# Product 4 of the W_base stage by seven inner products over two pairs, in an adaLN and feed-forward kernel

## The chip, the cores and the metric

The kernel runs on one core of a Trainium2 chip. The metric is device time in microseconds (us), the median of the runs. Engines: PE is TensorE (matmuls), DVE is VectorE, ACT is ScalarE, POOL is GpSimd, SP is SyncE (here it only issues transfers).

## The reference

For each of 16 batches of 512 tokens by 1024 features:

```
q_emb = relu(cond @ W3 + b3)
n, v_sum = tokens, sum of x over tokens
c = relu(((n * x + v_sum) * q_emb) @ W2 + b2)                # stage 1, 1024 x 1024
base   = c @ W_base + b_base                                 # stage 2, 1024 x 1024
shared = (c @ A_s) @ B_s                                     # rank 16
gates  = softmax(c @ W_router + b_router), the best 2 of 6 kept
routed = sum over e of gate_e * (c @ A_r[e]) @ B_r[e]        # rank 16 each
out = x + base + shared + routed
```

Everything is float32. Each matmul operand is split into a rounded part (hi) and the rest (lo), both float32r, and each product is three matmuls: hi by hi, hi by lo, lo by hi (`three`, L2390 to L2394).

## The kernel before, in words

Two batches make a pair, eight pairs in all; a pair's 1024 x 1024 by 1024 x (2 x 512) product is one block product of 2 x 2 by 2 x 2 blocks, done by Strassen-Winograd's seven block products, numbered 0 to 6, instead of eight. Both stages do that: `g` 0 to 7 are the pairs of the first stage (W2), `g` 8 to 15 those of the second (W_base), where p = g - 8. A block product `group(g, n, j)` for j = 0 to 3 has four groups, one for each 128 output features; a group is 4 x 3 = 12 matmuls into one PSUM bank. In stage 2 the rank-16 parts join as `low_rank`: three matmuls more at the end of a group of products 4, 5 and 6. Their four output blocks are C11, C12, C22, C21; C11 is made of products 0 and 1, and its low-rank rows have a place of their own: `low_rank_c11` (L2610) writes them to a bank, and DVE adds the bank (`c11_add_low`, L2178).

In pairs 2 to 7 of both stages product 1 isn't done pair by pair. Two neighbouring pairs have the same weight block there, so the two blocks of data are put side by side, and that wider product is again cut in two each way and done by seven inner products (`inner(e, m)`, L2548: 12 matmuls each, m = 0 to 6) instead of two block products of 48 matmuls. They are done in the even pair (g = 2, 4, 6 and 10, 12, 14, the list `QUADS`); the odd pair only adds what was kept for it (`partner`). Inner weight sets are quarters of W and their sums, split in hi and lo. There is no room to keep them on the core; they are written once to HBM by way of a staging buffer of two slots, and each is loaded again, 512 KB, before its inner product into one of two slots (`inner_w`).

How a weight set is made: ACT rounds it (`inner_weight_high(c)`, L1026; c counts the sets, 0 to 6 for W2, 7 to 13 for W_base, and after the change 14 to 20), having waited until set c - 2 is stored; DVE makes the rest (`inner_weight_low(c)`, L1813); four sums on DVE make the sets 3 to 6 of a kind (`inner_weight_sums`, L1818); POOL's queue stores it (`store_weights`, L720). For W_base this is done in the last pair before the first even one, g = 9 (`SECOND - 1`).

What sets the order: it is written out by hand. Each engine has one instruction stream, waits are on semaphores, and an engine never passes a waiting instruction. POOL's stream in stage 2 is: the seven stores; then for each even pair the first two weight sets (`begin`), the other pair's data (`load_partner`, two loads of 512 KB), and the five sets m = 2 to 6 (`stream`), each waiting until inner product m - 2 is done. PE's order in an even pair (`even`, L2637): four groups of product 0 and three of product 2, each followed by an inner product, and the last group of product 2; then products 3 (with `low_rank_c11` after each group), 4, 5 and 6. ACT rounds operands (`high`, L827) and copies banks (`copy_p0`, `copy_u2`, `copy_u4`); DVE makes the low parts (`low`, L1511), the operand sums (`t1` to `t4`) and the outputs (`add_bank`, L1594).

## Time and profile before

| | |
|---|---|
| time of the runs | 1394.6 us (median of 3; 1394.54 to 1394.91) |
| span of the profiled execution | 1392.4 us |
| the median less that span | 2.2 us (no time of the profiled execution itself beside its span is given) |
| PE busy | 1388.2 us, 100% of the span, 6105 matmuls |
| DVE, ACT, POOL busy | 71%, 46%, 4% |
| granted PE clock | 1.00 in every slice |
| transfers | 237.8 MB, 171 GB/s on average |

A profiled matmul is shown with a duration of 0.39 us, but matmuls overlap: what counts is the distance from the start of one to the start of the next. In the same way DVE's and ACT's instructions overlap a little, so a chain of them goes by distances between starts. The number in brackets at the end of a timeline row is how long the engine stood idle before it, and what it waited for.

### The profile page before, as it was taken

To read this page: it belongs to the slowest core of one execution; us is meant where nothing else is said; L and a number is where in the kernel's file an instruction comes from. 1 tells how busy PE (TensorE), PEld (TensorE's weight loads), DVE (VectorE), ACT (ScalarE), POOL (GpSimd) and SP (SyncE) were. 2 spreads that over 40 slices of the span, in tenths; PEclk is the share of its full clock that TensorE was granted. 3 is DMA by queue.
4 is the path that set the end of the run, shared out by engine and by line. 5 is a ranking of instruction groups with operands and counts; after the bars stand their busy time and mean duration, and the time that the engine had idled before them with its cause. 6 is when DMAs were issued, how large, how long until landed. Compare 5 with 4: busy or idle time off the path is not lost.

```text
span 1392.4 us, 18247 instructions
## 1 busy us (share of the span) xinstructions
PE 1388.2 (100%) x6105; PEld 1142.9 (82%) x6105; DVE 986.5 (71%) x1648; ACT 644.2 (46%) x1190; POOL 60.7 (4%) x136
## 2 busy tenths in 40 slices
PE   9999999999999999999999999999999999999999
PEld 6888888888888888888888888888888888888887
DVE  6987777676786757768889667766667656586663
ACT  7774756657465564655544232431314313243130
POOL 3000110000000000000000001000000000000000
PEclk9999999999999999999999999999999999999999
DMA  8243836445264452546836549556463665635542
GB/s 318 75 168 113 263 122 182 156 122 165 62 184 153 122 165 61 171 130 211 285 92 195 212 132 342 176 190 226 146 239 114 203 213 167 218 107 175 211 155 87
DMA packets 146429, 237.78 MB, mean 171 GB/s; under 512 B 39872, under 2 KB 40128, under 8 KB 146336
## 3 DMA queue, kind: packets, MB, share of 16 engines
q1 hardware_dynamic: 135680, 199.75, 43.6%
q0 software_dynamic: 9792, 35.66, 8.3%
q10 hardware_dynamic: 864, 1.22, 0.2%
...
## 4 chain that ended last, share of the span: by engine, by line
PE 100%; DVE 0%; DVEq 0%; issue 0%
PE ps L2392 33%; PE ps L2393 33%; PE ps L2394 33%; PE ps L2403 1%; PE ps L2418 0%; PE ps L2412 0%; DVE buf L2385 0%; DVEq L59 0%; DVE zeros L1708 0%
## 5 line engine op out<-in xcount | busy, mean ns | idle before, releaser
L2392 PE MATMUL ps<-act_hi,w_hi 128*128 128x512 f32 x1600 | 623.0, 389 | 0.0
L2393 PE MATMUL ps<-act_lo,w_hi 128*128 128x512 f32 x1600 | 622.8, 389 | 0.0
L2394 PE MATMUL ps<-act_hi,w_lo 128*128 128x512 f32 x1600 | 622.8, 389 | 0.0
L2392 PEld LDWEIGHTS ps<-act_hi,w_hi 128*128 128x128 f32 x1600 | 300.4, 188 | 63.1 <-DVE act_lo L1520 0.9
L2393 PEld LDWEIGHTS ps<-act_lo,w_hi 128*128 128x128 f32 x1600 | 300.4, 188 | 62.3
L2394 PEld LDWEIGHTS ps<-act_hi,w_lo 128*128 128x128 f32 x1600 | 300.4, 188 | 62.2
L854 ACT ACTIVATE act_hi<-src 128x512 fp32r<-128x512 f32 x232 | 140.5, 624 | 152.6 <-PE ps L2394 151.5
L1595 DVE SCALAR_TENSOR_TENSOR buf<-ps,bb_sb,buf 128x512 f32<-128x512 f32 x115 | 85.6, 748 | 125.6 <-PE ps L2394 100.7
L1527 DVE TENSOR_TENSOR act_lo<-src,act_hi 128x512 fp32r<-128x512 f32 x192 | 130.2, 685 | 23.8 <-ACT act_hi L854 23.6
L873 ACT ACTIVATE yhi<-buf 128x512 fp32r<-128x512 f32 x128 | 80.1, 626 | 81.3 <-PE ps L2394 80.9
L1595 DVE SCALAR_TENSOR_TENSOR buf<-ps,b_sb,buf 128x512 f32<-128x512 f32 x80 | 59.4, 748 | 43.8 <-PE ps L2394 43.7
L1520 DVE SCALAR_TENSOR_TENSOR act_lo<-src,shift,act_hi 128x512 fp32r<-128x512 f32 x104 | 76.6, 747 | 18.8 <-ACT act_hi L851 18.8
L851 ACT ACTIVATE act_hi<-src,shift 128x512 fp32r<-128x512 f32 x100 | 69.9, 715 | 11.4 <-PE ps L2394 9.4
L854 ACT ACTIVATE act_hi<-buf 128x512 fp32r<-128x512 f32 x64 | 39.0, 627 | 71.5 <-DVE buf L1560 61.7
L1650 DVE TENSOR_TENSOR buf_lo<-buf,yhi 128x512 fp32r<-128x512 f32 x64 | 43.4, 687 | 37.9 <-ACT yhi L873 37.8
L895 ACT ACTIVATE buf<-ps 128x512 f32<-128x512 f32 x64 | 37.5, 592 | 68.3 <-PE ps L2394 68.1
L906 ACT ACTIVATE buf<-ps 128x512 f32<-128x512 f32 x60 | 35.7, 596 | 70.7 <-PE ps L2394 70.6
L808 ACT ACTIVATE src<-src,qn 128x512 f32<-128x512 f32 x92 | 65.4, 711 | 2.8 <-DMA src<-in_xT 2.8
L2393 PE MATMUL ps<-act_lo,inner_w 128*128 128x512 f32 x168 | 65.4, 389 | 0.0
L2394 PE MATMUL ps<-act_hi,inner_w 128*128 128x512 f32 x168 | 65.4, 389 | 0.0
L2392 PE MATMUL ps<-act_hi,inner_w 128*128 128x512 f32 x168 | 65.4, 389 | 0.0
L1527 DVE TENSOR_TENSOR act_lo<-buf,act_hi 128x512 fp32r<-128x512 f32 x64 | 42.4, 685 | 19.0 <-ACT act_hi L854 18.9
...
## 6 DMA issues: line engine op xcount, KB each, us to landing
...
y_scratch<-buf SPq DMA_DIRECT2D x128, 256.0 KB, 3.1
src<-y_scratch SPq DMA_DIRECT2D x128, 256.0 KB, 5.2
...
```

The source lines that it names most:

```text
L808: nc.scalar.activation(src[:, t, :], src[:, t, :], ACT.Identity, scale=qn[:, H * HALF_OF[q] + k, 2 * i + BATCH_OF[q]:2 * i + BATCH_OF[q] + 1],
L851: nc.scalar.activation(act_hi[:, slot(g, n, k), :], source[:, t, :], ACT.Identity, bias=shift[:, t:t + 1]).then_inc(hi_done, 1)
L854: nc.scalar.activation(act_hi[:, slot(g, n, k), :], source[:, t, :], func).then_inc(hi_done, 1)
L873: nc.scalar.activation(yhi[:, (y_no(i, c, j) - 1) % 2, :], buf[:, j, :], func).then_inc(yhi_done, 1)
L895: nc.scalar.activation(buf2[:, j, :], ps[:, j, :], ACT.Copy).then_inc(u2_copied, 1)
L1520: nc.vector.scalar_tensor_tensor(act_lo[:, s, :], source, shift[:, t:t + 1], act_hi[:, s, :].bitcast(F32), ALU.add, ALU.subtract).then_inc ...
L1527: nc.vector.tensor_tensor(act_lo[:, s, :], source, act_hi[:, s, :].bitcast(F32), ALU.subtract).then_inc(lo_done, 1)
L1595: nc.vector.scalar_tensor_tensor(buf, ps[:, bank, :], bias, buf, ALU.add, ALU.add).then_inc(done, 1)
L1650: nc.vector.tensor_tensor(lo, y, hi, ALU.subtract).then_inc(ylo_done, 1)
L2392: nc.tensor.matmul(out, wh, a_h, start=start, stop=False, skip_group_check=onto)
L2393: nc.tensor.matmul(out, wh, a_l, start=False, stop=False, skip_group_check=onto)
L2394: return nc.tensor.matmul(out, wl, a_h, start=False, stop=stop, skip_group_check=onto)
```

## The change

- Product 4 of pairs 2 to 7 of stage 2 is done for two pairs at once, as product 1 is. Each even pair has two runs of seven inner products, r for product 1 and f for product 4; the weight sets of product 4 are a third kind (c = 14 to 20), stored and loaded as the others are. The raw quarters come from adding hi and lo of the W_base block that is on the core (`raw_four`).
- The low-rank rows of C11 (even pairs) and of C12 (both pairs) no longer ride on a group of product 4 or on a bank of their own: in an even pair inner products 1 and 5 of either run have six low-rank matmuls more, that accumulate in the inner product's banks (`with_low`); in an odd pair `low_rank_c12` adds three matmuls into the bank of each group of product 3, after ACT has copied it.
- C12 of the even pair is gathered in a new buffer (`acc4`), whose x rows SP loads ahead; product 4 of the odd pair waits in `partner4`, loaded by POOL.
- The orders of all engines in the even pairs are written anew, and in pair g = 9 and at the start of g = 10 the making of sets 14 to 20 is put in.

The diff, cut to its core:

```diff
+        def four_joined(g):
+
+            return g >= NP and joined(g)
+
+        RUNS = [(e_of, n_of) for e_of in range(len(QUADS)) for n_of in ((1, 4) if e_of >= EARLY else (1,))]
+        RUN = {key: r_of for r_of, key in enumerate(RUNS)}
+
...
-                if n_of != 1 or not joined(g_of):
+                if not (n_of == 1 and joined(g_of)) and not (n_of == 4 and four_joined(g_of)):
...
+            def load_x12(p):
+                for j in range(H):
+                    if p > 2:
+                        sp.wait_ge(buf1_stored[j], 16 * 2 * (NP + p - 1))
+                    else:
+                        sp.wait_ge(inner_w_lo, 3 * L2)
+                    sp.dma_start(acc4[:, j, :], xT[2 * p + 1, j]).then_inc(x12_loaded[j], 16)
...
+            def inner_weights(r, m):
+                e, n = RUNS[r]
+                c = L2 * r + m
+                kind = 2 if n == 4 else int(e >= EARLY)
                 if m < 2 and e in (0, EARLY):
-                    for r in range(2):
-                        pool.wait_ge(inner_w_stored[r], 16 * ((L2 * (late + 1) + 1 - r) // 2))
+                    weights_stored(kind)
                 if c >= 2:
                     pool.wait_ge(inner_done, 2 * (c - 1))
-                pool.dma_start(inner_w[:, c % 2], inner_dram[late, m]).then_inc(inner_w_loaded[c % 2], 16)
+                pool.dma_start(inner_w[:, c % 2], inner_dram[kind, m]).then_inc(inner_w_loaded[c % 2], 16)
+
+            def load_partner4(e):
+                g = QUADS[e] + 1
+                if e == EARLY:
+                    weights_stored(2)
+                for h in range(2):
+                    if e > EARLY:
+                        pool.wait_ge(c12_done, four(QUADS[e] - 1, 2 * h + 1))
+                    for k in (2 * h, 2 * h + 1):
+                        pool.wait_ge(buf3_stored[k], 16 * (g - NP + 1))
+                    pool.wait_ge(partner_loaded[h], other_loaded_no(RUN[e, 1]))
+                    pool.dma_start(partner4[:, 2 * h:2 * h + 2, :],
+                                   y_dram[2 * (g - NP) + 1, H + 2 * h:H + 2 * h + 2].rearrange("k p t -> p k t")
+                                   ).then_inc(partner_loaded[h], 16)
 
             def load_partner(e):
                 g = QUADS[e] + 1
...
                         for k in (2 * h, 2 * h + 1):
                             pool.wait_ge(buf2_stored[k], 16 * (g - NP + 1))
                         from_dram = y_dram[2 * (g - NP), H + 2 * h:H + 2 * h + 2]
+                        pool.wait_ge(partner_loaded[h], other_loaded_no(RUN[e, 1] - 1))
                     pool.dma_start(partner[:, 2 * h:2 * h + 2, :], from_dram.rearrange("k p t -> p k t")
...
             for e in range(EARLY, len(QUADS)):
-                begin(e)
+                begin(RUN[e, 1])
                 load_partner(e)
-                stream(e)
+                if e == EARLY:
+                    for c in range(2 * L2, 3 * L2):
+                        store_weights(c)
+                load_partner4(e)
+                stream(RUN[e, 1])
+                begin(RUN[e, 4])
+                stream(RUN[e, 4])
 
...
+                a_max(r)
+                inner_high(r, 0)
+                inner_high(r, 1)
+                if e == EARLY:
+                    inner_weight_high(3 * L2 - 2)
                 copy_p0(g, 0)
-                inner_high(e, 2)
+                lr_high_a(p)
+                inner_high(r, 2)
                 copy_p0(g, 1)
-                inner_high(e, 3)
                 copy_p0(g, 2)
-                inner_high(e, 4)
+                if e == EARLY:
+                    inner_weight_high(3 * L2 - 1)
                 for j in range(H):
                     high(g, 2, j)
+                a_max(f)
...
-                    if g == SECOND - 1 and j in (0, 2):
-                        inner_weight_high(L2 + 5 + j // 2)
-                if p < LAST:
-                    for j in range(H):
-                        high(g + 1, 0, j)
+                    if g == SECOND - 1 and j in (0, 1):
+                        inner_weight_high(L2 + 5 + j)
+                    elif g == SECOND - 1:
+                        inner_weight_high(2 * L2 + j - 2)
+                for j in range(H):
+                    high(g + 1, 0, j)
+                    if g == SECOND - 1 and j > 0:
...
+            def raw_four():
+
+                dve.wait_ge(bank_done, group_no(SECOND - 1, 4, H - 1))
+                for k in (0, 2):
+                    nc.vector.tensor_tensor(wl_raw[:, 4, k:k + 2, :], w_lo[:, 4, k:k + 2, :].bitcast(F32),
+                                            w_hi[:, 4, k:k + 2, :].bitcast(F32), ALU.add).then_inc(inner_w_sum, 1)
 
...
+                r, f = RUN[e, 1], RUN[e, 4]
+                inner_low(r, 0)
+                inner_t1(r)
+                inner_low(r, 1)
+                inner_t2(r)
+                if e == EARLY:
+                    inner_weight_low(3 * L2 - 2)
+                lr_low_a(p)
+                add_p0(r, 0)
+                inner_low(r, 2)
+                inner_t3(r)
+                add_p0(r, 1)
+                if e == EARLY:
+                    inner_weight_low(3 * L2 - 1)
+                add_p1(r, 0)
+                add_p1(r, 1)
...
+                if g == SECOND - 1:
+                    raw_four()
...
+                    if g == SECOND - 1 and j == 1:
+                        inner_weight_low(2 * L2 + 2)
+                        inner_weight_sums(2)
+                    elif g == SECOND - 1 and j > 1:
+                        inner_weight_low(2 * L2 + 1 + j)
...
+                with_low = e >= EARLY and m in (1, 5)
+                    inner_free(r, m, jt)
+                        s = inner_slot(r, m) + kk
+                                   act_hi[:, s, :], act_lo[:, s, :], kk == 0 and not onto, kk == 1 and not with_low,
+                                   onto)
+                    if not with_low:
+                        mm.then_inc(inner_done, 1)
+                if with_low:
+
+                    p = QUADS[e] - NP
+                    hi, lo = (ha_hi, ha_lo) if n == 1 else (hb_hi, hb_lo)
+                    pe.wait_ge(lr_lo_done, 3 * p + (2 if n == 1 else 3))
+                    for jt in range(2):
+                        j = jt + (2 if m == 5 else 0)
+                        cols = slice(j * P, (j + 1) * P)
+                        three(ps[:, B_BANKS[jt], :], low_hi[:, cols], low_lo[:, cols], hi[:, :], lo[:, :], False, True,
+                              onto).then_inc(inner_done, 1)
...
 
+            def low_rank_c12(p, j):
+
+                pe.wait_ge(u4_copied, four(NP + p, j))
+                if j == 0:
+                    pe.wait_ge(lr_lo_done, 3 * p + 3)
+                cols = slice(j * P, (j + 1) * P)
+                three(ps[:, j, :], low_hi[:, cols], low_lo[:, cols], hb_hi[:, :], hb_lo[:, :], False, True,
+                      True).then_inc(lr_done, 1)
...
+                r, f = RUN[e, 1], RUN[e, 4]
+                group(g, 0, 0)
+                inner(r, 0)
+                group(g, 0, 1)
+                group(g, 0, 2)
+                inner(r, 1)
+                group(g, 0, 3)
+                inner(r, 2)
+                group(g, 2, 0)
+                inner(r, 3)
+                group(g, 2, 1)
+                inner(r, 4)
+                group(g, 2, 2)
+                inner(r, 5)
+                inner(r, 6)
+                group(g, 2, 3)
+                for j in range(H):
+                    group(g, 3, j)
+                    inner(f, j)
+                for j in range(H):
+                    group(g, 5, j, (1, 3 * (g - NP) + 3, hb_hi, hb_lo))
+                    if j < H - 1:
+                        inner(f, H + j)
+
+            def odd(p):
+                g = NP + p
                 for j in range(H):
                     group(g, 0, j)
+                for j in range(H):
                     group(g, 2, j)
+                    low_rank_c11(p, j)
+                group(g, 3, 0)
+                group(g, 3, 1)
+                low_rank_c12(p, 0)
+                group(g, 3, 2)
+                low_rank_c12(p, 1)
+                group(g, 3, 3)
+                low_rank_c12(p, 2)
+                low_rank_c12(p, 3)
+                for j in range(H):
+                    group(g, 5, j, (1, 3 * p + 3, hb_hi, hb_lo))
```

Three places where the streams are different. First POOL, from the stores of the W_base weight sets to the first even pair (`staged_w`, in the changed kernel `staged_1`, is the staging buffer, `inner_scratch` its copy in HBM, `inner_w` the two slots that PE reads). Before:

```order
L722 DMA inner_scratch<-staged_w 128x1024 [waits inner_w_lo] x7
L733 DMA inner_w<-inner_scratch 128x1024 [waits inner_done,inner_w_stored1,inner_w_stored0] x2
L746 DMA partner<-y_scratch 128x2x512 [waits buf2_stored1,buf2_stored0]
L746 DMA partner<-y_scratch 128x2x512 [waits buf2_stored3,buf2_stored2]
L733 DMA inner_w<-inner_scratch 128x1024 [waits inner_done] x7
```

And now:

```order
L848 DMA inner_scratch<-staged_1 128x1024 [waits inner_w_lo] x7
L864 DMA inner_w<-inner_scratch 128x1024 [waits inner_done,inner_w_stored1,inner_w_stored0] x2
L892 DMA partner<-y_scratch 128x2x512 [waits partner_loaded0,buf2_stored1,buf2_stored0]
L892 DMA partner<-y_scratch 128x2x512 [waits partner_loaded1,buf2_stored3,buf2_stored2]
L848 DMA inner_scratch<-staged_4 128x1024 [waits inner_w_lo] x7
L876 DMA partner4<-y_scratch 128x2x512 [waits buf3_stored1,buf3_stored0,partner_loaded0,inner_w_stored1,inner_w_stored0]
L876 DMA partner4<-y_scratch 128x2x512 [waits partner_loaded1,buf3_stored3,buf3_stored2]
L864 DMA inner_w<-inner_scratch 128x1024 [waits inner_done] x5
L864 DMA inner_w<-inner_scratch 128x1024 [waits inner_done,inner_w_stored1,inner_w_stored0] x2
```

Between the loads for inner products 0 and 1 and the loads for 2 to 6 there now stand seven stores, each waiting for DVE, and two loads of `partner4`, the first of which waits until all stores have landed.

Second ACT, from the operands of product 6 in pair g = 9 to the first inner operand of g = 10 (`act_hi<-src 128x512` are operands of groups, `act_hi<-src 128x1024` those of inner products, `staged` the weight sets). Before:

```order
L854 ACTIVATE act_hi<-src 128x512 [waits op_used,t4_made]
L1348 ACTIVATE ha_hi<-hd 128x512 [waits lr_done,hd_made]
L854 ACTIVATE act_hi<-src 128x512 [waits op_used,t4_made]
L1034 ACTIVATE staged_w<-wl_raw 128x512 [waits inner_w_stored1,inner_w_sum,wl_loaded1]
L854 ACTIVATE act_hi<-src 128x512 [waits bank_done,t4_made]
L854 ACTIVATE act_hi<-src 128x512 [waits op_used,x_loaded0]
L854 ACTIVATE act_hi<-src 128x512 [waits op_used,x_loaded1]
L854 ACTIVATE act_hi<-src 128x512 [waits op_used,x_loaded2]
L854 ACTIVATE act_hi<-src 128x512 [waits bank_done,x_loaded3]
L1045 ACTIVATE src<-src 128x1024 [waits x_loaded13,x_loaded12]
L1103 ACTIVATE act_hi<-src 128x1024 [waits op_used,a_ready]
```

And now:

```order
L1193 ACTIVATE staged_1<-wl_raw 128x512 [waits inner_w_stored1,inner_w_sum,wl_loaded1]
L1010 ACTIVATE act_hi<-src 128x512 [waits op_used,t4_made]
L1193 ACTIVATE staged_4<-wl_raw 128x512 [waits inner_w_stored0,inner_w_sum]
L1010 ACTIVATE act_hi<-src 128x512 [waits bank_done,t4_made]
L1193 ACTIVATE staged_4<-wl_raw 128x512 [waits inner_w_stored1,inner_w_sum]
L1010 ACTIVATE act_hi<-src 128x512 [waits op_used,x_loaded0]
L1010 ACTIVATE act_hi<-src 128x512 [waits op_used,x_loaded1]
L1193 ACTIVATE staged_4<-wl_raw 128x512 [waits inner_w_stored0,inner_w_sum]
L1010 ACTIVATE act_hi<-src 128x512 [waits op_used,x_loaded2]
L1193 ACTIVATE staged_4<-wl_raw 128x512 [waits inner_w_stored1,inner_w_sum]
L1010 ACTIVATE act_hi<-src 128x512 [waits bank_done,x_loaded3]
L1193 ACTIVATE staged_4<-wl_raw 128x512 [waits inner_w_stored0,inner_w_sum]
```

Six rows for weight sets stand between operands that PE needs, each with a wait for a store (`inner_w_stored`); before it was one.

Third DVE, at the end of pair g = 9 and in the first even pair (`act_lo<-src,act_hi 128x512` are operands of groups). Before:

```order
L1527 TENSOR_TENSOR act_lo<-src,act_hi 128x512 [waits hi_done]
L1595 SCALAR_TENSOR_TENSOR buf2<-ps,bb_sb,buf2 128x512 [waits bank_done,u2_copied]
L1543 TENSOR_TENSOR src<-src 128x512 [waits x_loaded2,x_loaded10]
L1527 TENSOR_TENSOR act_lo<-src,act_hi 128x512 [waits hi_done]
L1595 SCALAR_TENSOR_TENSOR buf2<-ps,bb_sb,buf2 128x512 [waits bank_done,u2_copied]
L1543 TENSOR_TENSOR src<-src 128x512 [waits x_loaded3,x_loaded11]
L1595 SCALAR_TENSOR_TENSOR buf2<-ps,bb_sb,buf2 128x512 [waits bank_done,u2_copied]
L1920 TENSOR_TENSOR act_lo<-src,act_hi 128x1024 [waits inner_hi_done]
```

And now:

```order
L1765 TENSOR_TENSOR src<-src 128x512 [waits x_loaded1,x_loaded9]
L2037 TENSOR_TENSOR staged_4<-wl_raw,staged_4 128x512 [waits inner_w_hi]
L2053 TENSOR_TENSOR wl_raw<-wl_raw 128x2x256 [waits inner_w_lo,inner_w_sum]
L2054 TENSOR_TENSOR wl_raw<-wl_raw 128x2x256
L2056 TENSOR_TENSOR wl_raw<-wl_raw 128x2x256 [waits inner_w_sum]
L2058 TENSOR_TENSOR wl_raw<-wl_raw 128x2x256 [waits inner_w_sum]
L1749 TENSOR_TENSOR act_lo<-src,act_hi 128x512 [waits hi_done]
L1817 SCALAR_TENSOR_TENSOR buf2<-ps,bb_sb,buf2 128x512 [waits bank_done,u2_copied]
L1765 TENSOR_TENSOR src<-src 128x512 [waits x_loaded2,x_loaded10]
...
L2037 TENSOR_TENSOR staged_4<-wl_raw,staged_4 128x512 [waits inner_w_hi]
L1817 SCALAR_TENSOR_TENSOR buf2<-ps,bb_sb,buf2 128x512 [waits bank_done,u2_copied]
L2163 TENSOR_TENSOR act_lo<-src,act_hi 128x1024 [waits inner_hi_done]
```

A weight set and the four sums stand ahead of the third operand of product 0, and one more weight set ahead of the last C21 row of the pair before and the first inner operand.

## Rows read from the trace of the kernel before

**Rows 1.** Page, busy times; then the waits of PE over the span.

```profile
PE 1388.2 (100%) x6105; PEld 1142.9 (82%) x6105; DVE 986.5 (71%) x1648; ACT 644.2 (46%) x1190; POOL 60.7 (4%) x136
...
PE ps L2418 <- DVE zeros L1708: 1.2, 1, 1.2
```

**Rows 2.** Timeline of PE: start us, duration us, engine, line, operation.

```profile
1.17 3.52 PE L2418 MATMUL ps<-zeros 128*128 128x512 bf16 x9 [1.17 <-DVE zeros L1708]
...
902.30 0.39 PE L2392 MATMUL ps<-act_hi,w_hi 128*128 128x512 f32 x1
...
905.02 0.39 PE L2392 MATMUL ps<-act_hi,inner_w 128*128 128x512 f32 x1
...
918.62 0.39 PE L2392 MATMUL ps<-ha_hi,low_hi 128*128 128x512 f32 x1
```

**Rows 3.** Timeline of POOL around the start of pair g = 10.

```profile
854.18 0.53 POOL L722 DMA_DIRECT2D inner_scratch<-staged_w  x1 [2.59 <-DVE staged_w L1815]
860.17 0.53 POOL L722 DMA_DIRECT2D inner_scratch<-staged_w  x1 [5.45 <-DVE staged_w L1815]
868.52 1.07 POOL L733 DMA_DIRECT2D inner_w<-inner_scratch  x2 [7.82 <-DMA inner_scratch<-staged_w]
869.57 1.49 POOL L746 DMA_DIRECT2D partner<-y_scratch  x2
881.13 0.55 POOL L733 DMA_DIRECT2D inner_w<-inner_scratch  x1 [10.07 <-PE ps L2394]
```

**Rows 4.** Landing times: the stores at 854.18 and 860.17, all 14 stores.

```profile
DMA to landing us min/median/max: 6.2/6.2/6.2
...
DMA to landing us min/median/max: 7.6/7.6/7.6
...
DMA to landing us min/median/max: 3.2/5.3/7.7
```

**Rows 5.** Landing times of loads: inner_w at 868.5, partner at 869.6, all 42 inner_w.

```profile
DMA to landing us min/median/max: 4.5/5.2/5.9
...
DMA to landing us min/median/max: 7.2/7.6/7.9
...
DMA to landing us min/median/max: 3.6/3.8/5.9
```

**Rows 6.** Windows: busy time by engine, clock, DMA share, GB/s.

```profile
865.00:870.00 5.00, 5.00 (x24) 4.14 (x23) 3.38 (x6) 1.06 (x1) 1.48 (x3) 1.00 1.08 403
895.00:900.00 5.00, 5.00 (x23) 4.14 (x23) 3.87 (x7) 1.62 (x4) 0.53 (x1) 1.00 0.27 86
```

**Rows 7.** Timeline of ACT: a weight set, operand of product 6, copy after product 3.

```profile
856.49 0.63 ACT L1034 ACTIVATE staged_w<-wl_raw 128x512 fp32r<-128x512 f32 x1 [4.87 <-DMA inner_scratch<-staged_w]
857.03 0.62 ACT L854 ACTIVATE act_hi<-src 128x512 fp32r<-128x512 f32 x1
...
918.82 0.60 ACT L906 ACTIVATE buf<-ps 128x512 f32<-128x512 f32 x1 [1.08 <-PE ps L2394]
```

**Rows 8.** Timeline of DVE from the last weight sets to the first inner operands.

```profile
834.86 0.68 DVE L1821 TENSOR_TENSOR wl_raw<-wl_raw 128x512 f32<-128x512 f32 x1
...
837.52 0.68 DVE L1527 TENSOR_TENSOR act_lo<-src,act_hi 128x512 fp32r<-128x512 f32 x1
...
852.55 0.74 DVE L1595 SCALAR_TENSOR_TENSOR buf<-ps,bb_sb,buf 128x512 f32<-128x512 f32 x1
853.21 0.68 DVE L1815 TENSOR_TENSOR staged_w<-wl_raw,staged_w 128x512 fp32r<-128x512 f32 x1
853.81 0.68 DVE L1527 TENSOR_TENSOR act_lo<-src,act_hi 128x512 fp32r<-128x512 f32 x1
...
875.37 0.75 DVE L1595 SCALAR_TENSOR_TENSOR buf<-ps,bb_sb,buf 128x512 f32<-128x512 f32 x1 [2.05 <-PE ps L2394]
876.03 1.22 DVE L1920 TENSOR_TENSOR act_lo<-src,act_hi 128x1024 fp32r<-128x1024 f32 x1
877.17 1.22 DVE L1866 SCALAR_TENSOR_TENSOR partner<-partner,src 128x1024 f32<-128x1024 f32 x1
...
887.02 2.49 DVE L1560 SCALAR_TENSOR_TENSOR buf<-src 128x512 f32<-128x512 f32 x4
```

723 lines of the change are left out of this document (489 added, 234 removed).

## The prediction, written before the changed kernel had run

> **What bounds the kernel now.** I read the page's busy times and PE's waits first [rows 1]: PE is busy for 1388.2 of 1392.4 us, and its one wait with a releaser is 1.2 us at the start. PE never waits for an operand, a bank or a weight set, so every matmul removed is time saved, and every microsecond that the change makes PE wait is time lost. Then PE's timeline [rows 2]: the matmuls at 902.30 and 905.02 are the first ones of neighbouring blocks of twelve, so a matmul costs 2.72 / 12 = 0.2267 us and a block 2.72. The one at 902.30 starts the eleventh block of pair g = 10 (four groups and four inner products of product 0's part, group 0 of product 2, inner product 4 before it), so that pair begins at 902.30 - 10 x 2.72 = 875.1; the DVE row at 875.37, which waits for the last group of pair 9, agrees [rows 8]. The granted clock is 1.00 in all windows, of which two are shown [rows 6]. After that I read the stretch from 850 to 905, where the third kind of weight sets is now made: POOL [rows 3], landings [rows 4, 5], ACT [rows 7] and DVE [rows 8]. The reader should see there that DVE and ACT have gaps but that the transfers are full: DMA share 1.08 at 403 GB/s between 865 and 870, against 0.27 between 895 and 900 [rows 6].
>
> **Matmuls.** For two joined pairs, product 4 was 2 x 48 matmuls and 2 x 12 low-rank ones, 120. Now it is 7 x 12 = 84, 12 low-rank ones in the even pair (inner products 1 and 5 of run f) and 12 in the odd (low_rank_c12), 108. C11's twelve are as many as before. Three times 12 go: 36 x 0.2267 = -8.2 us. This term is sure, 0.6% of the time.
>
> **The weight sets of product 4, and where they are late.** Everything else depends on the hand-over from g = 9 to g = 10. POOL now issues the loads for inner products 0 and 1 and for partner, then seven stores, each after DVE has made its set, then (after all have landed) partner4, and only then the load for inner product 2. In the new PE order inner product 2 comes after g00, inner 0, g01, g02, inner 1 (18 matmuls) and g03 (gnj is group j of product n): 5 x 2.72 + 4.08 = 17.7 us into the pair, at 892.8 on the old time axis. When does its weight set land? I follow sets 12 to 20.
>
> Step 1. DVE's C12 row at 852.55 and the set at 853.21 [rows 8] are now parted by raw_four, two operations on 1024 columns (1.14 us each, the distance 876.03 to 877.17), and an operand; set 12 starts at 856.1, and its store is issued 0.97 later (853.21 to 854.18 [rows 3]). Landings there took 6.2 and 7.6 us [rows 4]: set 12 lands at about 864.0, and set 13, stored at 858.9, at 866.2. ACT rounds set 14 only then (it waits for set 12), and behind it stands the last operand of product 6, whose high part was made at 857.03 [rows 7] and is now made at 864.6; DVE's part ends at 865.9. PE wants it 11.6 us before g = 10 (a group with low rank is 15 matmuls, 3.4 us; four of them less three quarters of the first's 12), at 863.5: 2.4 late.
>
> Step 2. POOL waits for set 13 (866.2), needs 2.56 us for four loads (868.52 to 871.06 [rows 3]) and issues the store of set 14 at 868.8, behind 2 MB of loads of its own. Partner took 7.2 to 7.9 us in that place [rows 5]; I take 8: 876.9. Set 16 waits for that on ACT, with two operands of g = 10's product 0 behind it. DVE then makes set 16, the four sums (2.66 us, 834.86 to 837.52 [rows 8]) and the third operand: ready at 881.6, with set 17 and the fourth at 884.0, where PE wants it at 877.1 unshifted. 7.0 late.
>
> Step 3. Set 18, the last C21 row and the low part of the first inner operand come after it on DVE: ready at 887.9, where it was 877.2 (876.03 + 1.22) [rows 8] and wanted at 877.8. 10.1 late.
>
> Step 4. From the start of that low part (886.7) DVE needs, to set 20: four operations of 1.14, set 19 and a low-rank part (0.60 each, as 853.21 to 853.81), a bank (0.66, as 852.55 to 853.21), two of 1.14, a bank, and four t2 in 2.4: 11.8 us. Set 20 starts at 898.5, its store at 899.5. The x rows of acc4 (four loads of 256 KB) wait for the same set and go beside it. With the median of all stores, 5.3 [rows 4], it lands at 904.8; partner4's two issues take 1.5 [rows 3]; the load of set 2 is issued at 906.3 and takes 5.2 as the pair of loads at 868.5 did [rows 5]: 911.5 against 892.8, so D = 18.7 us late in all.
>
> Bounds of D. If every store lands in 3.2 and the load in 3.6 [rows 4, 5], steps 1 to 3 vanish in DVE's gaps and set 20 starts at 887.8: 888.8 + 3.2 + 1.5 + 3.6 = 897.1, D = 4.3. If all take 7.7 and 5.9, the first inner operand starts at 888.5 and D is 23.6. Nothing makes D less than 4.3 as long as POOL's stream stands as it does, for all the terms are in series. I take D = 17, between, near the upper side, since steps 1 and 2 lie in the full stretch and step 4 in the empty one.
>
> The page "DMA: Bandwidth & Descriptors" of the Trainium skill (section on the anatomy of a POOL-issued DMA) gives a fixed 2.0 us and bytes / 436e3 for one transfer, an estimate of 3.2 us for 512 KB; the shortest row agrees, the median of 5.3 doesn't. By that page alone D would be near the lower bound of 4.3 and the kernel 3 us faster, the low edge of rival 2 below; the landings under load decide for the rows.
>
> **PE after a long wait.** The trace shows PE slow only at its start: nine matmuls in 3.5 us, 0.38 each instead of 0.2267 [rows 2], 1.4 us lost, though the granted clock reads 1.00 there too. After the wait at inner product 2 (some 7 us) I add the same 1.4; the bounds are 0 and three times that, as there are several waits.
>
> The page "TensorE: Matmul & The Clock Gate" of the Trainium skill (Part 1) says that the array falls to 1.2 GHz when idle and that activity releases it; a stretch at half clock costs its own half. No row of this trace shows a fall.
>
> **The odd pairs.** In low_rank_c12 the fourth trio waits for ACT's copy of the bank that the group just before finished; only the third trio, 0.68 us, lies between. A copy starts 0.20 after a group's end (918.62 to 918.82) and lasts 0.60 [rows 2, 7]: at least 0.12 us of waiting, with the hand-over back to PE about 0.25, bounded by 0 and 0.5. Three odd pairs: +0.8.
>
> **The even pairs' new second half.** The first operand of run f is rounded after inner product 6, two copies, two operands and copy_u2; counting from the end of that product with 0.2 to start and ACT's starts 0.5 to 0.6 apart, DVE's part is ready 5.1 us after it where PE wants it at 5.4 (groups g23 and g30). DVE itself comes there with 13 operations and six wide ones after inner product 4, 14 us of 14.9. Nothing waits, by 0.3 us: I take 0, bounds 0 and 3 us per even pair. Behind it on DVE stand c12's banks, which PE wants 10 us later, so a small slip isn't passed on. SP's acc4 loads wait for set 20 with nothing behind them that is due before product 3. The two later even pairs have no weight sets to make, and partner4 waits only for the odd pair's C12 rows, done in product 6 and before inner product 2 by over 17 us.
>
> **Sum.** 1392.4 - 8.2 + 17.0 + 1.4 + 0.8 = 1403.4 of span. The runs' median is 2.2 above the profiled span: 1405.6 us, 0.8% slower.
>
> **Rivals.**
> 1. The sets are in time, and only the matmuls count: 1394.6 - 8.2 + 0.8 = 1387.2, faster. For it: DVE was idle 2.05 us before 875.37 [rows 8], and sets 14 to 18 could slip in. Against it: store, partner4 and load in series behind set 20 need 8.3 us even at the shortest landings, and PE leaves 4. It needs an order on POOL that isn't there. 9%.
> 2. Short landings: the stretch is emptier than before because DVE's own lateness spreads the transfers, D = 4.3 to 10 and no slow restart: 1394.6 - 8.2 + 0.8 + 7.5 = 1394.7, within 0.2%. For it: the median of inner_w is 3.8. Against: two of the three links lie behind other transfers. 12%.
> 3. The even pairs' second half waits too: if DVE's slack of 0.3 us is an error of one wide operation and hand-overs, each of three pairs loses 1 to 3 us, 1405.6 + 5 = 1410.6. It decides where run f's first operand is later than g30's end. 10%.
> 4. The sharp side of steps 1 to 3, D = 23.6 with a second slow restart: 1405.6 + 6.6 + 1.4 = 1413.6. 6%.
> The rest, 63%, is the forecast, with its own range of 1398 to 1411.
>
> **Chances.** A measurement of this kernel can tell 0.2%, 2.8 us, from no change. Faster (under 1391.8): rival 1 and the low edge of rival 2, 12%. Within: the rest of rival 2, 10%. Slower 78%. The range of 1391 to 1412 leaves out rival 1 and most of rival 4.
>
> **What would show it.** Right: PE matmuls 36 fewer; PE idle in one piece of 5 to 10 us before inner product 2 of g = 10, released by a load of inner_w; shorter waits for act_lo at the last operand of product 6 in g = 9 and at g00 and inner 0; POOL idle until a landing of inner_scratch just before partner4; waits of 0.1 to 0.5 us for ACT's copies in three odd pairs. The span from 910 to the end is then shorter by about 7 us than before. Wrong: POOL's load for inner product 2 issued before 889; a PE without waits at 892; or waits of over 1 us in pairs 12 and 14, which none of my terms has.

## The result, and the profile after

| | before | after |
|---|---|---|
| time of the runs | 1394.71 us (4 runs; 1394.54 to 1394.91) | 1412.28 us (4 runs; 1411.66 to 1414.27) |
| ratio | | 1.0126, 95% interval 1.0112 to 1.0141 |
| profiled execution: time, span | span 1392.4 us | 1414.27, 1412.4 us |
| PE matmuls | 6105 | 6069 |
| granted clock, mean | 1.00 | 0.992 |

The kernel is 1.3% slower, where 0.8% was forecast, and the time lies 0.3 us outside the range. The profile's busy line of the changed kernel (before: [rows 1]):

```profile
PE 1388.9 (98%) x6069; PEld 1139.6 (81%) x6069; DVE 1037.6 (73%) x1700; ACT 664.0 (47%) x1209; POOL 79.5 (6%) x170
```

36 matmuls fewer, as counted, and yet PE is busy 0.7 us longer. So there is more to find than waits. The waits of PE (us in total, times, longest), against the single 1.2 of [rows 1]:

```profile
PE ps L2760 <- issue: 8.7, 1, 8.7
PE ps L2760 <- DVE act_lo L1749: 8.5, 3, 7.2
PE ps L2760 <- DVE act_lo L2163: 2.0, 1, 2.0
PE ps L2786 <- DVE zeros L1930: 1.2, 1, 1.2
```

Five places stop PE, all at the hand-over from g = 9 to g = 10. PE's timeline there, which answers to [rows 2]:

```profile
864.45 0.50 PE L2760 MATMUL ps<-act_hi,w_hi 128*128 128x512 f32 x1 [0.46 <-DVE act_lo L1749]
...
884.93 0.80 PE L2760 MATMUL ps<-act_hi,w_hi 128*128 128x512 f32 x1 [7.25 <-DVE act_lo L1749]
...
887.40 0.79 PE L2760 MATMUL ps<-act_hi,w_hi 128*128 128x512 f32 x1 [0.81 <-DVE act_lo L1749]
...
891.05 0.80 PE L2760 MATMUL ps<-act_hi,inner_w 128*128 128x512 f32 x1 [2.01 <-DVE act_lo L2163]
...
917.06 0.77 PE L2760 MATMUL ps<-act_hi,inner_w 128*128 128x512 f32 x1 [8.68 <-issue]
...
921.04 0.63 PE L2760 MATMUL ps<-act_hi,inner_w 128*128 128x512 f32 x1
921.46 0.63 PE L2761 MATMUL ps<-act_lo,inner_w 128*128 128x512 f32 x1
```

The five rows with brackets are the last operand of product 6, g00's third and fourth operand, inner product 0 and inner product 2. Measured from start to start and less one matmul's 0.2267, they stop PE for 0.62, 7.40, 1.22, 2.41 and 8.84 us: 20.5 in all. The last has no engine as its releaser; the load issued at 910.62 (below) landed 6.3 us later, at 916.9, and that is what it waited for. The last two rows are 0.42 us apart where full speed is 0.2267: after the waits PE goes on at about half speed. The windows (columns: stretch, length, PE, PEld, DVE, ACT, POOL busy, granted clock, DMA share, GB/s), two of 10 us and then three short ones, against the 1.00 of [rows 6]:

```profile
880.00:890.00 10.00, 3.30 (x6) 1.67 (x6) 9.10 (x15) 5.88 (x8) 1.55 (x3) 0.59 0.43 156
...
910.00:920.00 10.00, 2.94 (x7) 2.42 (x8) 2.25 (x3) 1.48 (x3) 1.75 (x3) 0.63 0.63 210
...
882.00:884.90 2.90, 0.00 (x0) 0.00 (x0) 2.83 (x6) 1.15 (x2) 0.36 (x1) 0.50 0.51 184
...
895.40:898.00 2.60, 2.60 (x12) 2.09 (x11) 1.96 (x3) 1.06 (x1) 0.53 (x1) 0.98 0.59 213
...
914.00:917.00 3.00, 0.00 (x0) 0.00 (x0) 0.00 (x0) 0.00 (x0) 0.00 (x0) 0.50 0.95 318
```

The granted clock falls while PE waits: it is at 0.50, the 1.2 GHz level, in the last 2.9 us before g00's third operand and in the last 3 us before inner product 2, stays there for the first matmuls, and is back at the 2.4 GHz level some matmuls later (0.98 from 895.4 on). The matmuls that are further apart than 0.2267 without being a wait cost 7.0 us together: about 3.3 from 884.9 to 895.5, 2.8 from 917.1 to 923, and 0.84 in the odd pairs (below). The account is then -8.2 + 20.5 + 7.0 = +19.3, and the span grew by 20.0.

POOL, which answers to [rows 3]; the row at 870.69 is the store of set 14, the one at 903.77 that of set 20:

```profile
868.19 1.06 POOL L864 DMA_DIRECT2D inner_w<-inner_scratch  x2 [6.78 <-DMA inner_scratch<-staged]
869.24 1.49 POOL L892 DMA_DIRECT2D partner<-y_scratch  x2
870.69 0.59 POOL L848 DMA_DIRECT2D inner_scratch<-staged  x1
...
903.77 0.53 POOL L848 DMA_DIRECT2D inner_scratch<-staged  x1 [7.81 <-DVE staged L2037]
909.17 1.45 POOL L876 DMA_DIRECT2D partner<-y_scratch  x2 [4.88 <-DMA inner_scratch<-staged]
910.62 1.13 POOL L864 DMA_DIRECT2D inner_w<-inner_scratch  x2
```

and the landings of the store at 870.69 and of the two loads at 910.62 (before: [rows 4, 5]):

```profile
DMA to landing us min/median/max: 9.3/9.3/9.3
...
DMA to landing us min/median/max: 6.3/6.7/7.0
```

ACT's rounding of set 13, which waited for the store of set 11 (issued at 852.04, landed 7.0 us later), and of set 16, which waited for the store at 870.69 (compare [rows 7]):

```profile
859.10 0.63 ACT L1193 ACTIVATE staged<-wl_raw 128x512 fp32r<-128x512 f32 x1 [6.76 <-DMA inner_scratch<-staged]
...
880.07 0.63 ACT L1193 ACTIVATE staged<-wl_raw 128x512 fp32r<-128x512 f32 x1 [10.88 <-DMA inner_scratch<-staged]
```

and DVE (compare [rows 8]): g00's third operand, the first inner operand, inner product 2's own operand, set 20.

```profile
884.19 0.68 DVE L1749 TENSOR_TENSOR act_lo<-src,act_hi 128x512 fp32r<-128x512 f32 x1
...
889.78 1.21 DVE L2163 TENSOR_TENSOR act_lo<-src,act_hi 128x1024 fp32r<-128x1024 f32 x1
...
897.33 1.22 DVE L2163 TENSOR_TENSOR act_lo<-buf,act_hi 128x1024 fp32r<-128x1024 f32 x1 [0.64 <-ACT act_hi L1273]
...
902.77 0.69 DVE L2037 TENSOR_TENSOR staged<-wl_raw,staged 128x512 fp32r<-128x512 f32 x1
```

This is the chain as forecast, link by link; from the second link on each is later than forecast. From inner product 2 to the last matmul the new kernel needs 1408.95 - 917.06 = 491.9 us, 489.1 without the slow restart, where it was 1388.95 - 892.8 = 496.2: 7.1 shorter, about what the matmuls less the odd pairs' waits give (8.2 - 0.8 = 7.4).

### The profile page after: what moved, and what is told of

Same layout as the page of the kernel before. It is cut to its first block and busy times, and to the rows that moved or that the text cites. A ratio compares the mean times of both kernels' runs of the same rounds, so it can differ in the third digit from the quotient of the medians.

```text
span 1412.4 us, 18365 instructions
## 1 busy us (share of the span) xinstructions
PE 1388.9 (98%) x6069; PEld 1139.6 (81%) x6069; DVE 1037.6 (73%) x1700; ACT 664.0 (47%) x1209; POOL 79.5 (6%) x170
## 3 DMA queue, kind: packets, MB, share of 16 engines
q10 hardware_dynamic: 864, 1.22, 0.2%
## 5 line engine op out<-in xcount | busy, mean ns | idle before, releaser
L2760 PE MATMUL ps<-act_hi,w_hi 128*128 128x512 f32 x1504 | 586.5, 390 | 8.5 <-DVE act_lo L1749 8.5
L2761 PE MATMUL ps<-act_lo,w_hi 128*128 128x512 f32 x1504 | 585.6, 389 | 0.0
L2762 PE MATMUL ps<-act_hi,w_lo 128*128 128x512 f32 x1504 | 585.6, 389 | 0.0
L2760 PEld LDWEIGHTS ps<-act_hi,w_hi 128*128 128x128 f32 x1504 | 282.7, 188 | 69.4 <-DVE act_lo L1749 10.1
L2762 PEld LDWEIGHTS ps<-act_hi,w_lo 128*128 128x128 f32 x1504 | 282.7, 188 | 58.7
L1817 DVE SCALAR_TENSOR_TENSOR buf<-ps,bb_sb,buf 128x512 f32<-128x512 f32 x91 | 67.4, 748 | 64.7 <-PE ps L2762 61.0
L2760 PE MATMUL ps<-act_hi,inner_w 128*128 128x512 f32 x252 | 100.4, 398 | 10.7 <-issue 8.7
L2762 PE MATMUL ps<-act_hi,inner_w 128*128 128x512 f32 x252 | 99.8, 396 | 0.0
L2761 PE MATMUL ps<-act_lo,inner_w 128*128 128x512 f32 x252 | 99.7, 396 | 0.0
L1062 ACT ACTIVATE buf<-ps 128x512 f32<-128x512 f32 x60 | 35.7, 594 | 66.6 <-PE ps L2762 66.5
L2760 PEld LDWEIGHTS ps<-act_hi,inner_w 128*128 128x128 f32 x252 | 48.4, 192 | 22.3 <-issue 9.1
```

The source lines that it names most:

```text
L1062: nc.scalar.activation(buf3[:, j, :], ps[:, j, :], ACT.Copy).then_inc(u4_copied, 1)
L1817: nc.vector.scalar_tensor_tensor(buf, ps[:, bank, :], bias, buf, ALU.add, ALU.add).then_inc(done, 1)
L2760: nc.tensor.matmul(out, wh, a_h, start=start, stop=False, skip_group_check=onto)
L2761: nc.tensor.matmul(out, wh, a_l, start=False, stop=False, skip_group_check=onto)
L2762: return nc.tensor.matmul(out, wl, a_h, start=False, stop=stop, skip_group_check=onto)
```

## The experiments

Each was timed beside the kernel before (1394.9 to 1395.3 us in the three groups of runs). The first four change the order of the hand-over, the next two the rest of the waits, and the last four take one term of the account each. "Wait" is from start to start less 0.2267, as above. The edits are shown cut to their core: lines taken out, unchanged lines around them and loop bounds that follow from them are mostly left out. The expectations speak of the changed kernel's time of 1412.3 us.

**1. The load for inner product 2 ahead of the last store.** POOL in the first even pair:

```diff
+ for c in range(2 * L2, 3 * L2 - 1): store_weights(c)
+ inner_weights(r, 2)
+ store_weights(3 * L2 - 1)
+ for m in (3, 4, 5): inner_weights(r, m)
+ load_partner4(e)
+ inner_weights(r, 6)
```

> The changed kernel, but in the first even pair (g = 10) POOL issues the load for inner product 2 before the store of set 20, the loads for 3 to 5 before partner4. Theory (the late load is what PE waits for, 8.8 us of idle and 2.9 us of matmuls 0.43 us apart behind it): the wait at inner product 2 goes, those at g00 and inner 0 stay, 1412.3 - 11.7 = 1400.6. Rival (inner product 2 is late anyway, its operand or its bank is next): under 3 us gained, 1409 or more.

Measured: 1401.28 us (1399.3 to 1401.68), ratio 1.0042 (1.0027 to 1.0057), 0.7 above the expectation. The waits in its trace, but for the one at the start:

```profile
PE ps L2768 <- DVE act_lo L1757: 6.0, 2, 5.1
PE ps L2768 <- DVE act_lo L2171: 2.0, 1, 2.0
```

The wait at inner product 2 and the slow matmuls after it are gone; those at g00 (5.3 in this execution) and inner 0 stay. So 11.0 us of the 17.6 hung on where the loads stand in POOL's order: that for inner product 2 ahead of one store, those for 3 to 5 ahead of partner4. The profiled execution is the fastest of the four (span 1397.5, 14.9 below the changed kernel's); 3.0 of its 14.9 are not the edit's, since its first loads on POOL went out at 865.70 instead of 868.19 and all up to inner product 0 came earlier with them.

**2. Sets 14 and 15 stored ahead of the even pair's loads.**

```diff
+ if e == EARLY:
+     store_weights(2 * L2)
+     store_weights(2 * L2 + 1)
  begin(RUN[e, 1])
  load_partner(e)
```

> The changed kernel, but POOL stores sets 14 and 15 before it loads the first two weight sets and partner. Theory (set 14 took 9.3 us to land because 2 MB of loads were ahead of it on POOL's queue, and ACT and DVE stood still for it): it lands within 6, the 7.4 us wait at g00 shrinks to under 2 and the slow matmuls behind it go, but the load for inner product 2 stays in series, so the gain is 6 to 11 us: 1401 to 1406. Rival (the transfers are full whoever is first): set 14 still lands after 8 us or more, 1410 or more.

Measured: 1408.64 us (1408.23 to 1409.02), ratio 1.0097 (1.0082 to 1.0112): neither the theory's 1401 to 1406 nor the rival's 1410. The wait at g00 shrank to 0.5, but a new one of 7.1 us stood at inner product 0, and that at inner product 2 stayed (8.4). ACT's timeline tells why the wait moved:

```profile
882.28 0.63 ACT L1196 ACTIVATE staged<-wl_raw 128x512 fp32r<-128x512 f32 x1 [7.18 <-DMA inner_scratch<-staged]
882.82 1.04 ACT L1211 ACTIVATE src<-src 128x1024 f32<-128x1024 f32 x1
883.89 1.06 ACT L1276 ACTIVATE act_hi<-src 128x1024 fp32r<-128x1024 f32 x1
```

The store that waits behind 2 MB of loads is now that of set 16; ACT stands before set 18 for it, and the operands of inner product 0 are queued behind. The lateness moved by two sets.

**3. Both.** The edits of 1 and 2 together.

> Both of the POOL orders together. Theory: what is left is DVE's and ACT's extra work at the hand-over, 0 to 5 us of waiting against 8.2 saved: 1388 to 1393, faster than before the change. Rival (the DVE chain of sums at the hand-over is late by itself): 1395 or more, with waits at g00 and inner 0 of over 5 us.

Measured: 1397.26 us (1395.43 to 1398.41, 10 runs), ratio 1.0016 (1.0006 to 1.0025): a miss again. The rival's time came, but not its cause. It had DVE's sums late, with waits at g00 too; in the trace the sums are done at 874.4 and g00 doesn't wait. One wait is left, of 7.7 us, at the same inner product 0, with ACT held as in 2 (7.4 us for the store of set 16). Neither order of POOL alone hides the chain: ACT's own order puts PE's operands behind sets that wait for stores.

**4. The sets moved into gaps, on all three engines.** No set later than 15 is made in g = 9. Sets 14 and 15 stand on ACT ahead of product 0's operands, 16 to 20 among the copies and operands behind inner product 1's; DVE follows. POOL in the first even pair:

```diff
+ if e == EARLY: store_weights(2 * L2)
  begin(r)
  load_partner(e)
+ store_weights(2 * L2 + 1)
+ inner_weights(r, 2)
+ for c in (2, 3, 4): store_weights(2 * L2 + c)
+ inner_weights(r, 3); inner_weights(r, 4)
+ store_weights(2 * L2 + 5); store_weights(2 * L2 + 6)
+ inner_weights(r, 5)
  load_partner4(e)
+ inner_weights(r, 6)
```

> The changed kernel with sets 14 and 15 made after the last operand of product 6, sets 16 to 20 and the sums after DVE's second operand sum in g = 10, and POOL's stores and loads in the order in which they are due. Theory (all of the loss is the hand-over): no wait over 0.5 us but the start's, and the three 0.3 us waits in the odd pairs: 1394.7 - 8.2 + 0.8 = 1387.3. Rival (the new even pairs cost more by themselves): over 1390.

Measured: 1388.54 us (1387.72 to 1391.08), ratio 0.9951 (0.9935 to 0.9968): faster than both kernels, and 1.2 above the expectation, which had no wait over 0.5. Its one wait over 1 us in the even pairs:

```profile
917.00 0.47 PE L2779 MATMUL ps<-act_hi,inner_w 128*128 128x512 f32 x1 [1.00 <-issue]
917.31 0.39 PE L2780 MATMUL ps<-act_lo,inner_w 128*128 128x512 f32 x1
```

The next matmul starts 0.31 later, the one after at full speed: a wait of 1.15 us brings no slow stretch. The profiled execution is the slowest of the four (1391.08), and its span of 1389.2 adds up: 1392.4 - 8.2 for the matmuls, 1.3 at inner product 6 with the matmuls behind it, 0.8 in the odd pairs, 0.2 at inner product 5, 1.2 at the kernel's start and 1.3 in two waits of the first stage (413.8 and 415.0), which the traces of 5 and 6 have as 0.2 or not at all. So the arithmetic of the change is worth the 6.4 us of the medians (4.5 to 9.1 by the interval), and by the rows what the matmul count says less these waits, if the sets are made where nothing is queued behind them.

**5. C12's fourth trio later.** On top of 4, in odd pairs:

```diff
- low_rank_c12(p, 3)
  for j in range(H):
      group(g, 5, j, (1, 3 * p + 3, hb_hi, hb_lo))
+     if j == 0: low_rank_c12(p, 3)
```

> The version with the weight sets in the gaps (1388.54 us), and in odd pairs the fourth low-rank trio of C12 moved behind the first group of product 5. Theory: the odd pairs' only loss is PE's wait for ACT's copy of the bank just finished, 0.27 us at each of three pairs (the distances of 0.34 and 0.39 at 1019.97 and 1020.31 in that version's trace); with a group of 3.4 us between it is gone: 1388.5 - 0.8 = 1387.7, and no matmul distance over 0.23 in the odd pairs. Rival: the wait moves with it to product 5's first group, or DVE gets C12 later and something behind waits: 1388.5, no change, or above.

Measured: 1389.55 us (1389.27 to 1390.65), ratio 0.9962 (0.9949 to 0.9974), no gain over 4. The trio waits no more, but the wait has moved to the group that now stands ahead of it, as the rival said. The last operand of product 5's first group, in the first odd pair:

```profile
1020.04 0.50 PE L2779 MATMUL ps<-act_hi,w_hi 128*128 128x512 f32 x1
1020.38 0.40 PE L2780 MATMUL ps<-act_lo,w_hi 128*128 128x512 f32 x1
```

The first of them starts 0.46 after the matmul before it, the second 0.34 later: 0.34 us lost where it was 0.27, and the same again in the other two odd pairs (1189.10, 1358.20). By the profile the weight load of that matmul waited for DVE's `act_lo`, and DVE's row for it ends at 1019.99. With one trio fewer ahead of it PE comes to that operand sooner than in 4, and waits for it instead of for ACT's copy. The time agrees with no gain, but alone it could not tell: 0.8 us is within what differs between executions.

**6. The load for inner product 6 ahead of partner4.** On top of 5:

```diff
- load_partner4(e)
  inner_weights(r, 6)
+ load_partner4(e)
```

> As the run before (weight sets in the gaps, fourth C12 trio later), and POOL's load for inner product 6 of the first even pair issued before partner4's two loads. Theory: partner4 waits until 910.10 for the last set's landing and the load of inner 6 stands behind it, issued at 911.55, which makes PE wait 1.15 us at inner product 6 (917.00). It waits by itself only for inner product 4's end, about 909: issued there it lands before 916 and the wait is gone, 1387.7 - 1.15 = 1386.5 us, PE without a wait after the start. Rival: partner4, 0.6 us later and behind another 512 KB, comes late for DVE's operand sum of product 4's inner products and makes a new wait of some 1 us: 1387.7.

Measured: 1389.81 us (1388.94 to 1390.92), ratio 0.9963 (0.9950 to 0.9975), no gain over 5, 3.3 above the expectation. The wait at inner product 6 is gone, but in 5 it was only 0.6 us. The rival's wait stands in its place: DVE waits for partner4, and PE for the last operand of product 3's first group, which is behind it on DVE (0.65 us, and 0.34 more at the inner product that follows):

```profile
915.00 1.23 DVE L2114 SCALAR_TENSOR_TENSOR partner<-partner,src 128x1024 f32<-128x1024 f32 x1 [1.01 <-DMA partner<-y_scratch]
...
PE ps L2779 <- DVE act_lo L1766: 0.5, 1, 0.5
```

The expectation also built on the gain of 5, which isn't there, and on the median of 4, whose four runs lie between 1387.72 and 1391.08. The three versions 4 to 6 can't be told apart.

**7. PE kept busy during the wait at inner product 2.** In the changed kernel, product 0's groups 0 to 2 are computed again, same values, same banks, ahead of g03:

```diff
  inner(r, 1)
+ if e == EARLY:
+     for j in range(3): again(g, j)
  group(g, 0, 3)
  inner(r, 2)
```

> The changed kernel with 36 matmuls more: in the first even pair, ahead of g03, three groups of product 0 are computed once more into their banks after these were copied. They fill 8.2 of the 8.8 us that PE waits for the weights of inner product 2. Clock theory: inner product 2 starts at 917.1 as before, since its load doesn't depend on PE, but its 13 matmuls that were 0.43 us apart are now 0.2267 apart: 2.9 us less, 1409.4. Rival A: the slow matmuls come from the transfers or the late load and not from PE's idle time: inner 2 at 917.1 and slow again, 1412.3. Rival B: the extra matmuls push something back on ACT or DVE that the load hangs on: over 1413.

Measured: 1410.64 us (1408.79 to 1411.28), ratio 1.0109 (1.0096 to 1.0123). 36 matmuls more and 1.6 us less than the changed kernel, between the theory's 1409.4 and rival A's 1412.3; the rows decide. PE's timeline at inner product 2:

```profile
915.71 0.47 PE L2760 MATMUL ps<-act_hi,inner_w 128*128 128x512 f32 x1 [1.42 <-issue]
916.01 0.39 PE L2761 MATMUL ps<-act_lo,inner_w 128*128 128x512 f32 x1
916.24 0.40 PE L2762 MATMUL ps<-act_hi,inner_w 128*128 128x512 f32 x1
```

and its window from 910 on:

```profile
910.00:920.00 10.00, 8.58 (x38) 6.78 (x38) 6.57 (x10) 5.97 (x8) 0.54 (x1) 1.00 0.48 164
```

Clock 1.00 where it was 0.63, and matmuls 0.23 apart where they were 0.43, although the load took no less from its issue (908.46) to its use. The slow matmuls come from PE's idle time, and cost 2.8 us in the changed kernel. (This execution's load was also issued 2.2 us earlier, at 908.46, because set 13 landed earlier; its span of 1408.4 has both, 1412.4 - 1.35 - 2.8 = 1408.2.)

**8. PE kept busy in both waits.** As 7 with a fourth repeated group, and the first three matmuls of g00 ten times more:

```diff
+ if (g, n, j, k) == (QUADS[EARLY], 0, 0, 0):
+     for _ in range(10): three(ps[:, bank, :], ..., True, True, False)
```

> The changed kernel with 36 + 12 matmuls as in the run before (the groups 0, 1, 2 and 0 of product 0 once more ahead of g03) and 30 more ahead of g00 (its first three, ten times more), which fill 6.8 of the 7.4 us that PE waits for g00's third operand. Clock theory: the matmuls from 884.9 to 895 are 0.2267 apart too, but inner product 2 still waits for its load until about 917, because that load's chain (stores, partner4, load on POOL) doesn't hang on PE: the 3.8 us won in front go into that wait, and the time is that of the run before, 1409.4. Rival: the chain behind PE's slow stretch moves with it, since DVE and ACT wait for PE's banks there: inner 2 at 913 to 916, 1406 to 1408, and part of the lateness of inner product 2 was the clock's.

Measured: 1411.82 us (1410.25 to 1413.43), ratio 1.0116 (1.0101 to 1.0132): a miss by 2.4. The first fill left two waits open, of 1.67 at g00's fourth operand and 2.86 at inner product 0, and that was enough:

```profile
887.18 0.50 PE L2760 MATMUL ps<-act_hi,w_hi 128*128 128x512 f32 x1 [1.50 <-DVE act_lo L1749]
...
890.83 0.79 PE L2760 MATMUL ps<-act_hi,inner_w 128*128 128x512 f32 x1 [2.69 <-DVE act_lo L2163]
891.43 0.63 PE L2761 MATMUL ps<-act_lo,inner_w 128*128 128x512 f32 x1
```

PE is slow from 890.83 on as in the changed kernel, so the fourth repeated group (2.7 us) was one too many: inner product 2 starts at 919.04 instead of 917.06, at full speed and without a wait: 1412.4 + 2.0 - 2.8 = 1411.6, the span measured. POOL's load for inner product 2 was issued at 910.67, as in the changed kernel (910.62), although g00's own slow matmuls were gone; those of inner product 0 were still there (2.3 us), so what the whole first slow stretch costs stays open.

**9. The store of set 14 between the even pair's loads.**

```diff
  begin(RUN[e, 1])
+ if e == EARLY: store_weights(2 * L2)
  load_partner(e)
```

> The changed kernel with one order changed on POOL: the store of set 14 stands before partner's two loads (1 MB) instead of behind them. Contention theory: in the changed kernel this store, issued at 870.69 behind 2 MB, took 9.3 us and set the start of set 16 (880.1), g00's third operand and all that comes after it. Issued at about 869.2 behind 1 MB it takes 6 to 7 and lands near 876: g00's wait falls from 7.4 to about 3.5, inner products 0 and 2 come 3.9 us earlier, 1412.3 - 3.9 = 1408.4. Rival: the transfers only trade places; the store of set 15, now behind all of it, lands at 882 and holds set 17 and with it the fourth operand: the g00 wait moves from the third operand to the fourth, 1411 to 1412.

Measured: 1409.07 us (1408.55 to 1409.63), ratio 1.0100 (1.0085 to 1.0115), 0.7 above the expectation. POOL's store, and ACT's set 16 that waits for it:

```profile
867.93 0.55 POOL L848 DMA_DIRECT2D inner_scratch<-staged  x1
```

```profile
875.64 0.63 ACT L1195 ACTIVATE staged<-wl_raw 128x512 fp32r<-128x512 f32 x1 [7.75 <-DMA inner_scratch<-staged]
```

7.7 us from issue to use with 1 MB ahead of the store, 9.4 with 2 MB; the wait at g00 falls to 3.7, and all that follows comes 4.4 to 4.6 us earlier (inner 0 at 886.62, inner 2 at 912.48), of which 1.3 are an earlier landing of set 13 (loads issued at 866.88). The span of 1406.7 is 5.7 below the changed kernel's: 4.6, and 1.2 because the matmuls after inner product 2's wait of 8.35 us lost only 1.5. In the rows the whole chain follows this one landing. A wait at g00's fourth operand grew from 1.2 to 1.7, the trace of the rival.

**10. The loads for inner products 2 and 3 behind all stores, ahead of partner4.**

```diff
+ for c in range(2 * L2, 3 * L2): store_weights(c)
+ for m in (2, 3): inner_weights(r, m)
  load_partner4(e)
+ for m in (4, 5, 6): inner_weights(r, m)
```

> The changed kernel with one order changed on POOL: the loads for inner products 2 and 3 stand behind the seventh store (set 20) but ahead of partner4. Theory (my step 4 in two links): of the wait at inner product 2, DVE's lateness up to set 20 is one part (store issued at 903.8) and the wait for its landing with partner4's two issues another (load issued at 910.6). This takes away the second alone: load issued at 904.3, landed after 5 to 6 us at 909.5 to 910, where PE could start inner 2 at 908.2: the wait falls from 8.8 to 1.3 to 2 us, and the slow matmuls after it go (2.9): 1412.3 - 7 - 2.9 = 1402.4. Rival: the load lands at the same time because the store of set 20 and acc4's x rows are in its way: a wait of 4 or more, 1407 or above.

Measured: 1408.87 us (1406.82 to 1409.71), ratio 1.0095 (1.0079 to 1.0112): the rival held. The load was issued at 904.90, 5.7 us earlier than in the changed kernel, but landed only 4.0 earlier. Its row among the transfers issued (the last number is us to landing), and inner product 2:

```profile
inner_w<-inner_scratch POOLq DMA_DIRECT2D x1, 512.0 KB, 8.1
```

```profile
913.04 0.60 PE L2767 MATMUL ps<-act_hi,inner_w 128*128 128x512 f32 x1 [4.21 <-DVE act_lo L2170]
```

904.90 + 8.1 = 913.0. The releaser named, DVE, is the wrong one: its row at 911.49 is a later inner product's operand that happened to end at 912.7; inner 2's own was done at 899.0. Between 908 and 912 the transfers were full:

```profile
908.00:912.00 4.00, 0.84 (x4) 0.38 (x2) 4.00 (x7) 3.85 (x6) 1.45 (x2) 1.00 1.04 359
```

The store of set 20, the x rows of acc4 (1 MB), inner 3's load and partner4 (1 MB) share them. Moving the load past partner4 alone buys 3.4 us, where experiment 1 buys 11.0 by moving it past the last store too.

## Why the prediction was wrong, and where it was right

**The direction and the mechanism held.** The forecast was slower, by one chain: stores on POOL behind loads, ACT and DVE's operands behind the sets, partner4 and the load of inner product 2 behind the last store. Experiment 1 took the last part of this chain away and 11.0 us with it. Experiment 4 has the same arithmetic with the sets out of the way, and what it still loses is 1.3 at inner product 6, 0.2 at inner product 5 and the odd pairs' 0.8: but for that, this chain is the whole loss. The terms of the sum in turn:

- **Matmuls, -8.2.** Right: 36 fewer, and 7.1 us shorter from inner 2 to the end together with the odd pairs.
- **Step 1, 2.4 late at product 6's last operand.** Too much: 0.62. Set 12 was stored at 856.17 and landed at 862.4, where I had 864.0. But set 13 was stored at 860.88 instead of 858.9, and POOL's loads began at 868.19, 2.0 later than my 866.2. That 858.9 was given without a working, and the link behind it is missing: ACT had waited 6.76 us to round set 13, until the store of set 11 had landed.
- **Step 2, 7.0 cumulated at g00's fourth operand.** 0.62 + 7.40 + 1.22 = 9.2 of waits; with the slow matmuls between them PE took it at 887.40 instead of 877.1, 10.3 late. The store of set 14 took 9.3 where I took 8 from the partner's rows in that place [rows 5]; DVE's third operand was ready at 884.9 against 881.6. Experiment 9 shows that this landing sets what follows.
- **Step 3, 10.1 at inner product 0.** 11.7 of waits; PE started it at 891.05 instead of 877.8, 13.2 late, with the first inner operand ready at 891.0 against 887.9.
- **Step 4, D: the term that failed.** Inner product 2 started at 917.06, so D = 24.3 where the rows had given 18.7 and I took 17. The 5.6 above the rows are: POOL's loads after set 13 2.0, set 14's landing 1.3, DVE's chain to set 20 (902.77 - 889.78 = 13.0 against 11.8) 1.2, and the load's 6.3 against 5.2, 1.1. Of DVE's 1.2, 0.64 is the bracket at 897.33: ACT's operand waited for inner product 0's end, which the slow PE had put off; 0.33 is DVE's idle time before 895.33, behind an ACT row that waited for the load of `ha_raw`. The other 1.7 is mine: I went below the sum of the nearest rows "since steps 1 and 2 lie in the full stretch and step 4 in the empty one", which is a reason for short landings in step 4 only, and experiment 10 shows that step 4 isn't empty. D also lies above the upper bound of 23.6. That bound took the longest landings of before, 7.7 for a store and 5.9 for the load, and the change made two longer ones: set 14's 9.3, behind the new order's 2 MB, and the load's 6.3, behind partner4.
- **Slow restart, +1.4.** The other step that failed. I took PE's slow start of the kernel, 9 matmuls, as the size of a restart [rows 2], and counted it once; but that start is at a granted clock of 1.00, and the stretches here are at 0.50. The trace has 14 distances that are too long after inner product 2's wait, 2.8 us, and another slow stretch of about 3.3 after g00's. Only the first stands in the sum in full: the other lies ahead of the wait for the load, and of it only what it put off on ACT (0.64, above) reaches the end for certain. Experiment 7 shows that the 2.8 come from PE's idling and not from the transfers. The size isn't fixed: after 8.4 us of waiting at the same place experiments 2 and 9 lost 1.5. The rule of the Trainium skill's page "TensorE: Matmul & The Clock Gate" (Part 1) that I cited as shown by no row, that the array falls to 1.2 GHz when idle, is borne out by the rows here: 0.43 us between matmuls against 0.2267, and a granted clock of 0.50 from 914 on.
- **Odd pairs, +0.8.** Right: 0.28 in each of three pairs. In the first of them the fourth trio starts 0.40 after the matmul before it, and its second matmul 0.34 after its first, instead of 0.2267. Experiment 5 shows that the size is right but the term isn't ACT's copy alone: with the copy out of the way PE waits as long for an operand of product 5.

```profile
1042.76 0.39 PE L2762 MATMUL ps<-hb_hi,low_lo 128*128 128x512 f32 x1
1043.16 0.50 PE L2760 MATMUL ps<-hb_hi,low_hi 128*128 128x512 f32 x1
1043.50 0.39 PE L2761 MATMUL ps<-hb_lo,low_hi 128*128 128x512 f32 x1
```

- **Second half of the even pairs, 0.** Right: no distance there is over 0.25 in any of the three pairs; rival 3 is out.

Together: 7.3 from D and 1.4 from the restart are 8.7 of the 9.0 us by which the span of 1412.4 exceeds my 1403.4. The profiled execution had 1.9 us beside its span where I took 2.2, and the median lies 2.0 below that execution, which is why the runs are off by 6.7 only. The range of 1391 to 1412 was also narrower than its own bounds: D = 23.6 and three restarts give 1405.6 + 6.6 + 2.8 = 1415.0.

**The rivals.** Rival 1 (all sets in time) and 2 (short landings) are out; the shortest landings, 2.9 to 3.6 us, were those of sets 16 to 19, from 881.83 on. The measured case is near rival 4, which had D = 23.6 and two restarts, 1413.6, at a chance of 6%. It deserved more, though not because all landings came out long: against the sum of the rows those of sets 12, 13 and 20 were up to 0.7 shorter (6.2, 6.6 and 4.9), set 14's and the load's 1.3 and 1.1 longer, and set 11's 7.0 wasn't in the sum. That the links are in series means that a long one is made good by nothing.
